# A vision-transformer tower on one core: who copies the class key's column of each head, and who evicts the query projections

## The reference, cut to what matters

```python
q, k, val = jnp.split(h @ W_qkv[i], 3, axis=-1)
kr = (r @ W_r[i]).reshape(s_len, H, DH)
AC = jnp.einsum('bqhd,bkhd->bhqk', q + u, k)
BD = jnp.einsum('bqhd,khd->bhqk', q + v, kr)
prob = jax.nn.softmax((AC + BD) * inv_sqrt_d, axis=-1)
vec = jnp.einsum('bhqk,bkhd->bqhd', prob, val).reshape(b, s_len, H * DH)
h = layer_norm(h + vec @ W_o[i], ln1_g[i], ln1_b[i])
ff = jax.nn.relu(h @ W_ff1[i] + b_ff1[i]) @ W_ff2[i] + b_ff2[i]
h = layer_norm(ff, ln2_g[i], ln2_b[i])
```

## Time and profile before

| what | value |
|---|---|
| median of 3 runs | 2916.02 us (2913.54 to 2921.79) |
| the profiled execution's own time | 2918.17 us |
| its span | 2916.3 us |
| PE busy, share of the span | 2389.1 us, 82% |
| DVE busy | 1790.9 us, 61% |
| ACT busy | 1625.7 us, 56% |
| POOL busy | 1194.8 us, 41% |
| one MIDDLE body, first L1328 to the next body's | 71.8 us |
| granted clock of TensorE, mean | 0.96 of full speed |

### The profile page before, as it was taken

The page is one execution under the profiler, slowest core; times in us unless marked ns, Lnnn a source line. Parts: engine busy times, 40 slices in busy tenths (PEclk is TensorE's granted clock), DMA queues, the critical chain, the costliest instruction groups (busy, mean ns, idle before and its releaser), DMA issues. The chain is left out here.

```text
span 2916.3 us, 71823 instructions
## 1 busy us (share of the span) xinstructions
PE 2389.1 (82%) x19980; PEld 1758.5 (60%) x19981; DVE 1790.9 (61%) x5286; ACT 1625.7 (56%) x5077; POOL 1194.8 (41%) x2202
## 2 busy tenths in 40 slices
PE   1179999998989999998899999989888888733885
PEld 0156666666666666666666666666666666522553
DVE  8656666666666666665566666656666666642332
ACT  2156666666556666665566666656666666611221
POOL 3045444444454444434444444445444444002002
PEclk9599999999999999999999999999999999966998
DMA  4453333334533333345433333444333333072002
GB/s 161 92 123 101 87 86 86 87 87 127 148 86 88 87 87 87 87 128 153 103 86 84 84 84 84 142 122 122 89 84 84 84 83 83 13 215 98 23 24 71
DMA packets 382076, 280.80 MB, mean 96 GB/s; under 512 B 44280, under 2 KB 359792, under 8 KB 380400
## 3 DMA queue, kind: packets, MB, share of 16 engines
q1 hardware_dynamic: 375344, 261.14, 34.5%
q10 hardware_dynamic: 4864, 12.68, 1.3%
q0 software_dynamic: 1600, 4.23, 0.5%
HBM read 119.44 MB, written 57.45 MB: 61 GB/s over the span
## 5 line engine op out<-in xcount | busy, mean ns | idle before, releaser
L1180 ACT ACTIVATE E<-E,nb 128x257 f32<-128x257 f32 x1024 | 516.8, 513 | 70.2 <-DVE nb L1339 69.9
L1339 DVE CUSTOM_DVE_ANT_0 E<-bk,cb 128x257 f32<-128x257 f32 x1024 | 394.7, 420 | 96.5 <-PE bk L993 79.2
L902 PE MATMUL bk<-hin,w_sb 128*128 128x257 f16 x3072 | 427.1, 276 | 14.6 <-ACT rel L1116 9.0
L949 PE MATMUL bk<-ident,E 128*128 128x128 f32 x2048 | 325.8, 282 | 91.1 <-ACT E L1180 70.6
L1305 DVE TENSOR_TENSOR pt<-bk,pt 128x512 f16<-128x512 f32 x512 | 354.3, 692 | 68.3 <-ACT pt L1167 56.6
L798 POOL TENSOR_SCALAR rq<-rel 128x257 f16<-128x257 f32 x256 | 104.6, 409 | 608.9 <-ACT rel L1116 607.9
L902 PEld LDWEIGHTS bk<-hin,w_sb 128*128 128x128 f16 x3072 | 298.8, 98 | 67.6 <-ACT rel L1116 14.2
L949 PEld LDWEIGHTS bk<-ident,E 128*128 128x128 f32 x2048 | 220.5, 141 | 175.5 <-DVE pt L1305 134.3
L1167 ACT ACTIVATE pt<-bk 128x512 f16<-128x512 f32 x512 | 308.0, 602 | 11.3 <-PE bk L949 11.3
L992 PE MATMUL bk<-kh,qs 128*128 128x257 f16 x1024 | 259.4, 278 | 43.1 <-DMA hin<-hd_dram 27.5
L993 PE MATMUL bk<-kl,qs 128*128 128x257 f16 x1024 | 258.3, 277 | 0.0
(11 more groups left out here) (270 smaller groups left out, 4748.7 us busy)
## 6 DMA issues: line engine op xcount, KB each, us to landing
qs<-rq SPq DMA_DIRECT2D x256, 128.5 KB, 3.4
kh<-rk SPq DMA_DIRECT2D x256, 128.5 KB, 3.3
kl<-rk SPq DMA_DIRECT2D x256, 128.5 KB, 3.5
wf<-in_w_dram SPq DMA_DIRECT2D x168, 128.0 KB, 2.1
w_split_dram<-wh SPq DMA_DIRECT2D x168, 128.0 KB, 2.2
wf<-in_we_dram SPq DMA_DIRECT2D x96, 128.0 KB, 2.1
we_split_dram<-wh SPq DMA_DIRECT2D x96, 128.0 KB, 1.7
w_sb<-w_split_dram SPq DMA_DIRECT2D x12, 1024.0 KB, 6.6
```

What stands on the lines that cost most here:

```text
L902: r = mm(bank[4 + s % 2][:, 0:S], wcol(a, C_QKV, k, 3 * HD, chunk_at(s)), hin[:, m, k, :], start=i == 0, stop=i == 5)
L949: r = pe.transpose(bank[2 + h % 2][:, (kt * QT + qt) * P:(kt * QT + qt + 1) * P], E[:, h % 2, qt, kt * P:(kt + 1) * P], ident[:, :])
L1180: act.activation(E[:, h % 2, qt, :], E[:, h % 2, qt, :], ACT.Exp, bias=nb[:, 2 * h + qt:2 * h + qt + 1], scale=-1.0, accum_out=sums[:, qt, ...
L1339: v.tensor_tensor_reduce(E[:, h % 2, qt, :], bank[qt][:, 0:S], cb[:, h, :], -SCORE, 3e38, ALU.add, ALU.min, nb[:, 2 * h + qt:2 * h + qt + ...
```

## The change

The copy of the class key's column moves from ScalarE's loop to GpSimd's, where it stands behind the split of the head's slot (`class_column`). Every second query eviction (slots 0, 4, 8 and 12) moves from ScalarE to VectorE, where a `take_q` of the same sum is added; slots 2, 6, 10 and 14 stay on ScalarE. The same holds for the eight slots ahead of the first body. The waits of VectorE and TensorE for `ecol_ok` stay as they were.

```diff
--- before.py
+++ after.py
@@ -862,6 +862,13 @@
                         pool.tensor_tensor(wh[:, i, 1, :], wf[:, i, :], wh[:, i, 0, :], ALU.subtract).then_inc(split_lo, 1)
                         c += 1
 
+            def class_column(at, h):
+
+                n = at.put(count, 32, 2 * h + 2)
+                pool.wait_ge(const_ok, CONST)
+                pool.wait_ge(e_ok, n)
+                pool.tensor_copy(ecol[:, :, h:h + 1], E[:, h % 2, :, CLS:S]).then_inc(ecol_ok, 1)
+
             for s in range(2 * NP):
                 split_projection(At(pool, 0), s)
 
@@ -870,6 +877,7 @@
                 for h in range(H):
                     for s in slots(h, kind):
                         split_projection(at1, s)
+                    class_column(at, h)
                     if h == 3 and kind.ln2:
                         ln2_newton(at)
                     if h == 4 and kind.ln2:
@@ -1157,7 +1165,7 @@
             act.dma_start(io["cc"].rearrange("(h s) -> h s", h=H), cc[:, :]).then_inc(cc_out, 16)
             class_v(first)
             load_position_term(first)
-            for s in range(0, 2 * NP, 2):
+            for s in range(2, 2 * NP, 4):
                 take_q(first, s)
             for u in range(4):
                 v_part(first, u)
@@ -1182,7 +1190,7 @@
                     if kind.closing and h < NP:
                         take_kr(atl, h)
                     for s in slots(h, kind):
-                        if s % 2 == 0:
+                        if s % 4 == 2:
                             take_q(at1, s)
                     if h == 1 and kind.ln2:
                         first_rstd(var2_done, at(1, 0), 7, ln2_ok, y2_ok)
@@ -1195,9 +1203,6 @@
                         p_part(at, h - 1)
                     if h == NP + 4 and kind.entry:
                         class_v(atl)
-
-                    act.wait_ge(e_ok, at(32, 2 * h + 2))
-                    act.activation(ecol[:, :, h:h + 1], E[:, h % 2, :, CLS:S], ACT.Copy).then_inc(ecol_ok, 1)
                 p_part(at, H - 1)
                 act.wait_ge(key_done, at(1, 1))
                 act.activation(pkr[0:H, 0, :, 0:IMG], bank[6][0:H, :].rearrange("p (t s) -> p t s", t=2), ACT.Copy).then_inc(key_hi, 1)
@@ -1259,6 +1264,14 @@
                 v.wait_ge(proj_lo, at(16, s - 1))
                 v.tensor_tensor(rel[:, s % 2, :], bank[4 + s % 2][:, 0:S], kr16[:, j - NP, :], ALU.add).then_inc(k_ok, 1)
 
+            def take_q(at, s):
+
+                j = chunk_at(s)
+                v.wait_ge(proj_done, at(16, s + 1))
+                if s or not isinstance(at.g, int) or at.g:
+                    v.wait_ge(proj_lo, at(16, s - 1))
+                v.tensor_scalar(rel[:, s % 2, :], bank[4 + s % 2][:, 0:S], 1.0, u16[:, j:j + 1], ALU.mult, ALU.add).then_inc(q_ok, 1)
+
             def v_part(at, u):
                 v.wait_ge(v_hi, at(4, u + 1))
                 tt, half = divmod(u, 2)
@@ -1294,8 +1307,11 @@
 
             first = At(v, 0)
             class_v(first)
-            for s in range(1, 2 * NP, 2):
-                take_k(first, s)
+            for s in range(2 * NP):
+                if s % 2:
+                    take_k(first, s)
+                elif s % 4 == 0:
+                    take_q(first, s)
             for u in range(4):
                 v_part(first, u)
             class_q(first)
@@ -1341,6 +1357,8 @@
                     for s in slots(h, kind):
                         if s % 2:
                             take_k(at1, s)
+                        elif s % 4 == 0:
+                            take_q(at1, s)
                     if h >= 2:
                         p_part(at, h - 2)
                     if h == 2 and kind.ln2:
```

## The result

The changed kernel takes 2984.87 us (median of 4 runs, 2972.67 to 2985.97), the kernel before 2916.68 us: a ratio of 1.022, 95% interval 1.0198 to 1.0242. It is slower, by 68 us where 53 were forecast. The span of the profiled execution grew from 2916.3 to 2984.1 us.

The account below looks back on a forecast made before the run. ScalarE was taken to set the head loop's pace. 24 MIDDLE and TAIL bodies +50.6, ENTRY +6.3, OPENING -2.0, FINAL -1.6 made +53.3 on 2918.2: 2971.5, expected median 2969 us, range 2920 to 2992 (chance 0.80).

Parts of the forecast that it names:

- the forecast was +53.3: Sum over all body kinds, in us, added to the profiled execution's 2918.2 to give 2971.5.
- the forecast of 2.11: MIDDLE body's head loop: ends 2.11 us later, since VectorE's reductions of heads 6, 7, 8 and 12 wait for GpSimd's column.
- The price of the copy, 0.24: GpSimd's queue: each column copy takes 0.24 us start to start, taken from the L835 copy; bounds 0 and 0.307.
- The handover, 0.11: From GpSimd's finish to VectorE's waiting operation: 0.11 us, read where GpSimd left slot 5.
- OPENING was forecast to gain 2.0 us: OPENING body: has none of the layer norm steps on GpSimd, so it takes the full gain, -2.0 us.
- the prediction's 1.625 a head: Head loop: VectorE sets the pace at 1.625 us a head instead of ScalarE's 1.75, if nothing else holds VectorE.
- The change touches nothing else in a body: Outside the head loop of a body: no effect, so the head loop was read by itself.
- GpSimd keeps up: Rival, head loop: columns are done before VectorE asks, 28 bodies x 2.0 = 56 us off, 2860 us; chance 0.07.
- The copy is far dearer than its size: Rival, GpSimd's queue: 0.47 us per column, a loss of 3.65 us a body, 3011 us; chance 0.07.
- The two cancel: Rival, head loop: copy hides wholly and slack absorbs most of 0.51 us a body, 2916 to 2926 us; chance 0.06.
- 2.0 a body had been worked out for both halves unhindered: Head loop: passing the pace from ScalarE to VectorE gains 0.125 x 16 = 2.0 us a body if nothing else held VectorE.
- The rule on evictions: VectorE's new query eviction: priced like the key eviction at 0.34 us, against the skill page's 393 ns for 257 columns.

Follow-up runs that it names:

- the two moved kernels: The full change with 44 run-once semaphore increments on VectorE ahead of the first body, 2938.24 us; the kernel before with 58 such increments, 2887.16 us.
- the spread: Query evictions on VectorE, column on ScalarE, 44 increments, plus second layer norm steps moved across later heads in MIDDLE and TAIL bodies, against the same without: 2852.86 us.
- the five kernels of the table: Before; the change; before with 12 increments in each body (2929.84 us); the change with 44 increments ahead of the first body; before with 58 there.
- the moved change: The full change plus 44 semaphore increments on VectorE, run once ahead of the first body: 2938.24 us.

## Why the prediction was right, and where it was not

**What held.** The side, the mechanism and its places. The loops of all bodies but FINAL sum to +54 us, FINAL's is 1.5 shorter, and the forecast was +53.3. Step by step in one MIDDLE body, forecast and measured: head 3 to 6 6.72 and 6.71 us, 6 to 7 2.76 and 2.61, 7 to 8 2.42 and 2.37, 8 to 12 7.56 and 7.62, 12 to 15 4.79 and 4.60.

**The cleaner comparison.** As built, before and after differ in more than the change does: late starts at the jump and, in some bodies, a lower clock. Between the two moved kernels the loops sum to +51.4 us and all the rest to +0.6. In a MIDDLE body followed by a MIDDLE the loop is 2.06 us longer (27.18 to 29.24); from the body's first VectorE operation to ScalarE's last exponential, which is what the forecast of 2.11 was about, it is 1.84 (29.24 to 31.08). The prediction's steps for VectorE's own head 15 had given 2.4 (26.88 for 24.47).

**The price of the copy, 0.24, was twice too high.** It measured 0.12 to 0.13. The prediction read the interval behind L835 as that instruction's own; the split behind L835 began 0.04 us after its end, the split behind a column begins 0.04 before. The 0.156 us that the prediction had set beside it from the Trainium skill's "GPSIMD Engine Reference" lies above the measured cost as well.

**The handover, 0.11, was three times too low.** It was read from an eviction that waits in the middle of a head. At the start of a head a register instruction ahead of the reduction carries the wait, and from the end of GpSimd's copy to the reduction it is 0.35 us. That the register instruction is the reason is argued from the two rows, no run tried it. By an estimate four such handovers a body cost about 1 us more and seven copies 0.8 us less: the two errors hid each other, and the close match of the steps above is in part luck.

**Heads 0 to 3 were taken as fixed, and nearly were.** In the body shown they took 4.95 us where they took 5.42, but that is no gain of the change: in the moved kernels they take 5.35 and 5.40. After a late start at the jump they are shorter, 4.95 us, and at the lower clock longer, 6.15 on average; over the twelve MIDDLE bodies as built the two cancel to 5.45 against 5.42.

**OPENING was forecast to gain 2.0 us and lost 0.6.** Its second step, head 1 to 2, stood 3.15 us where it took 2.00, at a granted clock of 0.67 over heads 0 to 3 where it was 0.82. From head 3 on it gained 0.54 (20.69 to 20.15), a quarter of what was forecast. With the query evictions alone, moved, that part takes 19.51 us, which is the prediction's 1.625 a head: there the pace was right, and the copy on GpSimd is what takes it away.

**"The change touches nothing else in a body" was false.** It touches the length of VectorE's loop body. The stretches gave +15 us, which is the distance between 2969 and 2985, and inside it stand -18 and +32. The prediction had no term for this, and that the sum of it stayed small enough to leave 2985 in the range is luck: the place alone was worth 47 us to one kernel and 30 to the other.

**The rivals.** "GpSimd keeps up" is excluded by the 81 waits. "The copy is far dearer than its size" is excluded by its 0.12 us. "The two cancel" needed a loss of at most 0.5 us a body; it was 2.0. The query half by itself does gain, 0.64 us a body in the moved kernels (27.18 to 26.54) where 2.0 a body had been worked out for both halves unhindered: GpSimd's splits held VectorE in head 7 as before, for 1.44 us. With the spread as well it is 1.6 (27.18 to 25.59).

**The rule on evictions.** VectorE's new eviction with a bias from SBUF lasts 0.48 us and takes 0.40 from start to start (1193.10 to 1193.50), not the 0.34 of the key eviction. The page "VectorE: DVE Perf Modes" of the Trainium skill, in its section on the TRN2 errata, gives 0.393; there the page was nearer than the row that I chose.

## What to carry to other kernels

A small operation costs what waits for it, so look at the engine that takes it at the moments when it is late, not at its mean load: GpSimd was busy 73% of the loop and was late in four heads. Before pricing a wait, take the handover from a row with the same kind of waiting instruction. Where an engine's loop body has some 300 instructions, as here, an edit of a dozen instructions can move tens of us at the jump in either direction; move the loop by instructions that run once, and compare both kernels where the first operation of a body waits for nothing but its data, before crediting or blaming an edit. And look at the clock of the stretch before giving a longer step to the code.

## What the runs showed of the hardware

- VectorE's loop body of 315 instructions stood 4.41 us at its start in the row shown, against 1.54 when the loop stood 44 instructions further on, and over 12 MIDDLE bodies the stretch is 3.0 us longer (46.50 against 43.50); the cost of the place was 47 us of 2985 for the full change, 30 us of 2917 for before.
- CLOSING, ENTRY and FINAL bodies and the first TAIL, entered without a jump, stood 1.53 or 1.54 us there in the five kernels of the table.
- The instruction queue's packets (200, 178, 127, 100) fall with the moved loops. That these packets are what VectorE waited for is supported by the moved kernels and not by the pair before and after; which instructions each packet brings was not tried.
- With the change as built, TensorE stood idle for over 2 us at each jump back to a MIDDLE body, and in 5 of 12 bodies its granted clock over heads 0 to 3 was 0.72, which made them 6.15 us where the seven at 1.00 took 4.95. In the moved kernels none of the twelve is below 1.00.
- A GpSimd copy of 128 x 2 f32 lasts 0.19 us and takes 0.12 of its queue.
- From the end of GpSimd's copy to VectorE's next operation it is 0.35 us where a register instruction carries the wait, and it was 0.11 where the operation itself did.
- The TAIL stretches of 45.4 us in the moved change, where the last has 43.5, are two things: about 1 us of idle time at each jump (2.33 to 2.55 against 1.54), and the first TAIL, whose piece ahead of head 0 is 3.74 us and the others' 0.38.
- Still open: why only some bodies fall to the lower clock, which place is best for a loop, and what makes up the rest of the 0.8 us that the copy alone costs the loop above the full change.
